# The softmax's maximum as a bias of ScalarE's exponential, in place of a subtraction on GpSimd, in a windowed-attention and expert block

## The reference

```python
xn = _layernorm(x)
qkv = xw @ qkv_w + qkv_b                       # xw: windows of 64 rows
attn = einsum('bnqhd,bnkhd->bnhqk', q, k) * scale + rel_pos_bias
attn = softmax(attn, axis=-1)                  # over the 64 keys of a window
out = einsum('bnhqk,bnkhd->bnqhd', attn, v) @ proj_w + proj_b
# experts: top-k rows by score, h = silu(xg @ W1) * (xg @ W3), y = h @ W2 * weight, scatter-add
```

## Time and profile before

| what | value |
|---|---|
| median of three runs | 2001.4 us (2001.19, 2001.4, 2004.64) |
| the profiled execution's own time | 1999.27 us |
| its span in the trace | 1997.5 us |
| PE busy | 1942.1 us, 97% |
| PEld, DVE, ACT, POOL busy | 1565.7, 1159.3, 647.2, 596.1 us |
| granted clock of PE, mean | 0.994 of full speed |

### The profile page before, as it was taken

How to read it: one execution, slowest core, us unless ns; L and a number is a source line. 1 busy time by engine, 2 the same in 40 slices (tenths; PEclk the granted TensorE clock), 3 DMA queues, 4 the chain that set the end, 5 groups by cost and what they waited for, 6 DMA issues and landing times.

```text
span 1997.5 us, 39467 instructions
## 1 busy us (share of the span) xinstructions
PE 1942.1 (97%) x16707; PEld 1565.7 (78%) x16707; DVE 1159.3 (58%) x1657; ACT 647.2 (32%) x953; POOL 596.1 (30%) x410
## 2 busy tenths in 40 slices
PE   7999999999999999989999999999999999999997
PEld 5787777777777777777888888888888888888886
DVE  7666678787778887777454346344543463435311
ACT  3323333332344443323332232332322323323321
POOL 2454545545444444532211220212112202121111
PEclk9999999999999999999999999999999999999999
DMA  7444456555532222134443343532433334324311
GB/s 196 113 129 129 125 166 176 156 166 174 153 95 81 86 83 81 62 99 138 109 136 85 77 107 90 127 79 59 136 84 77 103 92 126 79 59 135 64 22 21
DMA packets 170608, 213.61 MB, mean 107 GB/s; under 512 B 31712, under 2 KB 103776, under 8 KB 170464
## 3 DMA queue, kind: packets, MB, share of 16 engines
q1 hardware_dynamic: 143456, 152.82, 26.8%
q0 software_dynamic: 14336, 33.56, 9.3%
q10 hardware_dynamic: 12672, 25.17, 3.4%
HBM read 127.08 MB, written 51.38 MB: 89 GB/s over the span
## 4 chain that ended last, share of the span: by engine, by line
PE 51%; DVE 1%; ACT 1%; SPq 1%; DMA 0%; issue 0%; POOL 0%; POOLq 0%
PE ps_e L59 17%; PE ps_e L60 17%; PE ps_e L61 17%; PE ps_e L157 1%; SPq L197 0%; DMA raw<-in_w 0%; ACT w_hi L1745 0%; DVE w_lo L1858 0%; DVE x_f L145 0%; DVE xn L1864 0%; POOL out_rows L1709 0%; DVE hm L1890 0%; DVE xgt_lo L1869 0%; DVE hot_v L136 0%; ACT x_res L1777 0%
## 5 line engine op out<-in xcount | busy, mean ns | idle before, releaser
L59 PE MATMUL ps_e<-xgt_hi,w_hi 128*128 128x512 f32 x1024 | 403.6, 394 | 0.1
L61 PE MATMUL ps_e<-xgt_hi,w_lo 128*128 128x512 f32 x1024 | 398.5, 389 | 0.0
L60 PE MATMUL ps_e<-xgt_lo,w_hi 128*128 128x512 f32 x1024 | 398.5, 389 | 0.0
L1890 DVE TENSOR_TENSOR hm<-ps_e,silu 128x512 f32<-128x512 f32 x128 | 88.4, 691 | 459.1 <-PE ps_e L61 458.2
L1709 POOL DMA_INDIRECT out_rows<-x_res,idx x64 | 100.6, 1572 | 429.8 <-ACT x_res L1777 415.4
L61 PEld LDWEIGHTS ps_e<-xgt_hi,w_lo 128*128 128x128 f32 x1024 | 192.2, 188 | 40.4
L59 PEld LDWEIGHTS ps_e<-xgt_hi,w_hi 128*128 128x128 f32 x1024 | 192.3, 188 | 38.3 <-DVE xgt_lo L1869 0.3
L60 PEld LDWEIGHTS ps_e<-xgt_lo,w_hi 128*128 128x128 f32 x1024 | 192.4, 188 | 37.8
L186 POOL DMA_INDIRECT x_in<-xn_rows,idx x64 | 77.1, 1204 | 479.2 <-DVE idx L178 307.5
L59 PE MATMUL ps<-xt_hi,wqk_hi 128*128 128x512 f32 x512 | 208.2, 407 | 4.5 <-issue 2.5
L1765 ACT ACTIVATE h_hi<-hm 128x512 fp32r<-128x512 f32 x128 | 80.9, 632 | 387.4 <-DVE hm L1890 385.0
(11 more groups left out here) (194 smaller groups left out, 3395.8 us busy)
## 6 DMA issues: line engine op xcount, KB each, us to landing
x_f<-in_w SPq DMA_DIRECT2D x48, 512.0 KB
raw<-in_w SPq DMA_DIRECT2D x48, 512.0 KB
x_res<-in_x SPq DMA_DIRECT2D x16, 1024.0 KB, 5.6
xn<-x_in SPq DMA_DIRECT2D x256, 64.0 KB, 2.0
pt<-pn_sb SPq DMA_DIRECT2D x248, 64.0 KB
out_rows<-x_res ACTq DMA_DIRECT2D x15, 1024.0 KB
xn_rows<-xt_plain SPq DMA_DIRECT2D x9, 1024.0 KB, 4.3
x_in<-xn_rows SPq DMA_DIRECT2D x28, 256.0 KB, 4.3
```

Source lines behind the costliest of these rows:

```text
L59: nc.tensor.matmul(out, w_hi, x_hi, start=start, stop=False)
L60: nc.tensor.matmul(out, w_hi, x_lo, start=False, stop=False)
L61: return nc.tensor.matmul(out, w_lo, x_hi, start=False, stop=stop)
L1890: v.tensor_tensor(hm[:, m % 2, :], ps[:, 2 * (m % 2) + 1, :], silu[:, m % 2, :], ALU.mult).then_inc(hm_ready, 1)
```

## The change

The subtraction on POOL is dropped at all its places. DVE's maximum is written negated, and ACT gives it as the bias of the exponential. A bias is one value for each partition, and `s_max` has 16 columns, so the one exponential of 1024 columns becomes 16 of 64 columns, each with its own column of `s_max`. ACT now waits for the maximum itself, and for `norm_ready` of the group before, since POOL must have read `p_sb` before it is written again; the order on POOL gave that before.

```diff
             def chunk(c):
                 s, n, j = G * c, c + 1, c + LEAD
-                subtract_max(s - 1)
                 if n < FAR:
                     layernorm_rstd(n)
                 normalise(s - 1)
...
             def exponentials(s):
-                act.wait_ge(sub_ready, s + 1)
-                nc.scalar.activation(p_sb[:, :, :, :], s_sb[:, :, :, :], ACT.Exp).then_inc(exp_ready, 1)
+                act.wait_ge(max_ready, s + 1)
+                if s >= 1:
+                    act.wait_ge(norm_ready, s)
+                for t in range(TT):
+                    for h in range(4):
+                        i = nc.scalar.activation(p_sb[:, t, h, :], s_sb[:, t, h, :], ACT.Exp, bias=s_max[:, 4 * t + h:4 * t + h + 1])
+                i.then_inc(exp_ready, 1)
...
                 dve.wait_ge(s_ready, s + 1)
-                nc.vector.tensor_reduce(s_max[:, :], s_sb[:, :, :, :].rearrange("p t h k -> p (t h) k"), AX.X, ALU.max).then_inc(max_ready, 1)
+                nc.vector.tensor_reduce(s_max[:, :], s_sb[:, :, :, :].rearrange("p t h k -> p (t h) k"), AX.X, ALU.max, negate=True).then_inc(max_ready, 1)
```

More of the change, by code:

```diff
@@ L319, in attention_block @@
         v_mm, v_ready = sem("v_mm"), sem("v_ready")
-        s_mm, s_ready, max_ready, sub_ready = sem("s_mm"), sem("s_ready"), sem("max_ready"), sem("sub_ready")
+        s_mm, s_ready, max_ready = sem("s_mm"), sem("s_ready"), sem("max_ready")
         exp_ready, sum_ready, rec_ready, norm_ready = sem("exp_ready"), sem("sum_ready"), sem("rec_ready"), sem("norm_ready")
@@ L509, in residual @@
                     nc.gpsimd.tensor_tensor(x_res[:, t, :], x_res[:, t, :], p_bias[:, :], ALU.add).then_inc(res_ready, 1)
[L511 to L515, removed]
             def normalise(s):
@@ L560, in chunk @@
                     residual(c - 1, (0, 1))
-                subtract_max(s)
                 normalise(s)
@@ L565, in chunk @@
                     weights_left(0)
-                subtract_max(s + 1)
                 normalise(s + 1)
@@ L573, in chunk @@
                     layernorm_rstd_ahead(j)
-                subtract_max(s + 2)
                 if c == NCH - 1:
@@ L590, in _ @@
                 chunk(c)
-            subtract_max(G * NCH - 1)
             residual(NCH - 1, (0, 1))
```

## The result

| | before | after |
|---|---|---|
| median of four runs, us | 2001.3 (1999.85 to 2004.64) | 2051.93 (2050.37 to 2053.03) |
| profiled execution, us; its span | 1999.27; 1997.5 | 2052.8; 2051.0 |
| ratio after to before | | 1.0253, 95% interval 1.0241 to 1.0266 |

The change costs 50.6 us, 2.5%. I forecast slower, at 2025, 23.4 us over before: the direction came true, the size is twice mine, and the time lies outside my range.

The account below looks back on a forecast made before the run. PE, busy 97% of the span, was taken as the bound, so only its waits counted. Added waits of 23.4 us on the median of 2001.4 gave 2024.8, say 2025 us, in a range of 2001 to 2048.

Parts of the forecast that it names:

- break-even near 3 us: Sixteen exponentials of a group taking 3.01 us together would end as late after the maximum as before the change.
- the last group counts in full: End of attention, group 63: the longer exponentials delay PE's transposes, with nothing else for PE to do, +2.5 us.
- relay: One group's way from the end of DVE's maximum to the exponentials' end: 3.08 us before, 3.69 forecast after.
- E: Time on ACT of one group's sixteen exponentials with bias, forecast at 3.62 us, with ends of 1.93 and 5.14.
- my sum: PE's added waits over attention: 6.5, 5.2 and 8.7 us in chunks 1 to 14, 2.5 and 0.5 elsewhere, 23.4 together.
- Group 22: start 324.27: In chunks 5 to 9, exponentials start 0.07 us after the maximum; DVE's sum then starts 0.6 us later than before.
- I take 220: Start-to-start time of the short exponentials on ACT, put at 220 ns among estimates of 224, 203 and 248.
- so their absence alone gives nothing: POOL's 122.9 us of subtractions end no other wait for PE, so removing them alone was held to gain nothing.
- rival A: On ACT the bias operand is fetched behind the piece before: pitch 112 ns, E 1.93 us, time 1997 us; chance 0.10.
- The place of absorption: Groups 25 and 26 of chunks 5 to 9: DVE's some 2 us of delay vanish in about 3 us of idle time.
- B: Exponentials on ACT don't overlap at all: E 5.14 us, 67 us on top, 2092 us; chance 0.05.
- C: The delays are absorbed beside PE's work, or E is near 3.0 us: 2001 to 2005 us; chance 0.12.

Follow-up runs that it names:

- Run 1: Changed kernel with ACT's store of the chunk before moved behind the exponentials of group s + 2: 2035.89 us, ratio 1.0173.
- run 2: Kernel before the change, with the store of the chunk before moved behind the exponentials of group s + 2: 2002.9 us, ratio 1.0009.
- run 3: Changed kernel with the sixteen exponentials kept but without their bias operand, the maximum computed but not subtracted: 1992.63 us, ratio 0.9953.
- run 4: Changed kernel with one exponential of 1024 columns and no bias, the maximum computed but not subtracted: 1976.76 us, ratio 0.9874.
- run 10: Changed kernel with the store behind the exponentials and eight maxima, each the bias of one exponential of 128 columns: 1984.16 us, ratio 0.9914.
- Run 8: Run 1's kernel with `k_part` put between the eighth and ninth exponential in three groups of a chunk: 2061.77 us, ratio 1.0312.
- run 5: Changed kernel with one maximum for a partition's 1024 scores as the bias of one exponential of 1024 columns: 1977.64 us, ratio 0.9883.

## Why the prediction was right or wrong

**Right.** That the exponentials' end decides, with break-even near 3 us; that a chunk has three of them in a row in its chain; that the last group counts in full; that the experts don't change. PE's transposes of the last group waited for that product, in the kernel after:

```profile
959.19 1.97 PE L894 MATMUL ps<-ident,pn_sb 128*128 128x128 f32 x8 [2.78 <-POOL pn_sb L518]
```

I had 2.5 there. The row before shows no wait at this place. The new wait for `norm_ready` costs nothing, as I said: no row of the exponentials' releasers names POOL. Run 1, whose relay is that of the change with the store out of the way, is a test of my walk: with E = 3.94 in place of 3.62 my sum is 23.4 + 0.32 x 3 x 14 + 0.3 = 37.1 us, and 34.6 was measured. That is nearer than it deserves: the sum has waits only, and some of the 34.6 is the clock's.

**Wrong, first: the store, 16.0 us.** The step was "Group 22: start 324.27". I moved the start of the exponentials up to the end of the maximum and asked only whether `q_part` or `o_hi_part` held ACT. Between `o_hi_part` and the exponentials stands `store_out`, with a wait for DVE and a DMA issue of 0.38 us; my sum has nothing for it. Busy time doesn't show it, since issues aren't counted as busy. For chunks 1 to 4 I even named `o_hi_part` as what held the start of group 10 until 163.56, and passed over the issue behind it. Run 1 puts the price at 16.0 us, and run 2 shows that nothing of it was visible before, because the subtraction covered it. It is what the removed operation had been hiding. Not all of it is waiting: of the 20.2 us between the profiled spans of the change and of run 1 (2051.0 and 2030.8), 6.9 are the clock's.

**Wrong, second: the pitch, about 13.7 us by my own walk.** The step was "I take 220" with E = 3.62; it measured 240 and 3.94. The 20 ns have three parts. A plain piece is 242 ns (run 3), and I had 230, drawn from two instructions of different functions; the operand is 93 against 91; together 14. The overlap is 95 ns against 97. The last 4 came off when I went from 224 down to 220, toward the copies that read PSUM. The page "ScalarE: Activation LUTs" of the Trainium skill (section "What ACT_TABLE_LOAD costs") gives figures from which I had worked out, as estimates, pitches of 146 and 240; run 3 (147) and the change (240) agree with them to 1 ns. The row of the copies, which seemed to speak against it, read another memory. Such a rule, stated for the very case, deserved a rival of its own.

**Wrong, third: two terms at nothing or nearly so.** The clock has no term in my sum, and it took 8.6 us more than before. And "so their absence alone gives nothing", like the 5 us that rival A gives a relay of 2.0 us, set the worth of a shorter relay far too low: run 4, with the subtraction gone and nothing in its place, gained 24.6 us, and run 10, with a relay of 2.52, gained 17.5. No run takes work off POOL and leaves the relay as it was, so what POOL's load alone is worth stays open.

The two, 16.0 and 13.7, with my 23.4 make 53.1; 50.6 was measured. That they meet so well is in part luck. With 8.6 us the clock's, the waits cost 42 us of the 50.6, or 45 of the 53.5 of span: the walk counted too many waits, and the clock, which it left out, made up for most of that.

**The place of absorption** was right for the wrong case. I let DVE's delay of 2 us vanish in the third group of a chunk. In groups 25 and 26 after the change it does: the sum is late by 18.5 us in group 25 against before, and the maximum of 26 by 17.4. But the uncovered store gave it back in the same group: the sum of group 26 is late by 19.4.

**Rival A** fell (the operand is paid in every piece), B too (neighbours overlap by 95 ns), and C too.

**Which part of the slope belongs to which waiter isn't settled.** Run 8 shows that `k_part` is not the only one, and that DVE's order behind the sum takes over at once. That a longer relay delays the next group's maximum can be read in the rows. This is the sum of group 24 after, and its transpose and the next maximum of the same kernel come later by the same amount, 17.23 us against before:

```profile
368.23 1.22 DVE L1212 TENSOR_REDUCE s_sum<-p_sb 128x16 f32<-128x1024 f32 x1 [3.41 <-ACT p_sb L639]
```

An order on DVE in which the transpose doesn't stand ahead of the next bias and maximum wasn't tried.

## What to carry to other kernels

When an operation is taken out of a relay, read the queue of the engine behind it, line by line, DMA issues and their waits included: what it ran beside is now in the open. Cutting one ACT instruction into n costs for every further piece what the pitch holds beyond its columns, and the operand in every piece. Here that was (2.45 - 1.06) / 15 = 0.093 us for each further piece and 0.093 for each operand. So ask first whether the operand must be that fine: here one constant for 16 softmax rows does the same as 16 (run 5, 74 us under the change), provided the maxima of the rows that share it lie close enough for the exponential's range. And a saturated main engine doesn't mean that a side engine's 1.9 us are hidden; run the removal alone, which showed 24.6 us here. And set the granted clock of both kernels side by side when waits of the main engine change: PE was slower for 17 us more of attention here, which no list of waits shows.

## What was not expected of the hardware

The start-to-start time of short ACT instructions depends on where they read: 128 by 64 from PSUM 112 ns (eight of them, before), from SBUF 147 ns (sixteen of them, run 3), both into SBUF and without an operand. There the functions differ too, a copy and an exponential. Two rows of the kernel before part the two, the same copy of 128 by 512, first from PSUM, then from SBUF:

```profile
48.16 2.04 ACT L616 ACTIVATE xt_hi<-ps 128x512 fp32r<-128x512 f32 x4
98.20 2.18 ACT L621 ACTIVATE xt_hi<-xt_plain 128x512 fp32r<-128x512 f32 x4
```

With 601 and 618 ns for the mean one, the pitches are (2.04 - 0.601) / 3 = 480 ns and (2.18 - 0.618) / 3 = 521 ns: 41 ns less from PSUM, where the short ones have 35 less. So it is the memory, and not the function.

An operand column from SBUF adds 93 ns to a piece and to its pitch alike, at 64 columns (335 against 242), and about 90 at 1024 (1149 against 1061).
